# Early loads split by rows, narrower evictions in the first two layers, and a reordered end of a four-layer conditional network

## The reference

```python
# layer 0: a base weight and a low-rank term of all experts, weighted by w = cond_8
out  = einsum('btc,oc->bto', x, W_base) + b_base
h    = einsum('btc,erc->bter', x, As)
x    = x + out + einsum('bter,eor,be->bto', h, Bs, w) * 2.0
# layer 1: a masked weight mixed over the experts
w_bot = einsum('bg,got->bot', cond_8, weight * mask)
x    = x + einsum('bnt,bot->bno', x, w_bot) + bias
# layer 2: gated MLP (128 -> 512 -> 128): one shared, and the top 2 of 8 experts by softmax(cond_8)
x    = x + mlp(x, shared) + sum_k w_k * mlp(x, expert_k)
mlp  = (gelu(x @ gate) * (x @ up)) @ down
# layer 3: gated MLP (128 -> 256 -> 128) of the expert argmax(cond_8)
x    = x + (silu(x @ Wu.T + bu) * (x @ Wg.T + bg)) @ Wd.T + bd
```

## Time and profile before

| what | value |
|---|---|
| three runs, us | 86.94, 88.13, 89.66 (median 88.13) |
| the profiled execution's own time | 87.69 us |
| its span (first to last instruction) | 85.9 us |
| TensorE matmul busy | 82.2 us (96%) |
| TensorE weight load busy | 77.3 us (90%) |
| VectorE, ScalarE, GpSimd busy | 47.3, 30.7, 15.6 us |
| DMA | 18.57 MB, mean 216 GB/s |

### The profile page before, as it was taken

How to read it: one execution, slowest core, us unless ns; L and a number is a source line. 1 busy time by engine, 2 the same in 40 slices (tenths; PEclk the granted TensorE clock), 3 DMA queues, 4 the chain that set the end, 5 groups by cost and what they waited for, 6 DMA issues and landing times.

```text
span 85.9 us, 1918 instructions
## 1 busy us (share of the span) xinstructions
PE 82.2 (96%) x618; PEld 77.3 (90%) x618; DVE 47.3 (55%) x109; ACT 30.7 (36%) x55; POOL 15.6 (18%) x20
## 2 busy tenths in 40 slices
PE   6899999999999999999999999999999999999980
PEld 6788977888888999999999999999999999999970
DVE  0278769743534998329328438446365564563270
ACT  4332692877556420221221221222302402407320
POOL 3020396097666900000000000000000000000000
PEclk9999999999999999999999999999999999999999
DMA  2996006889960000686889889989998979726102
GB/s 12 349 418 256 0 0 183 303 296 402 404 241 10 0 0 4 197 268 272 229 301 342 255 265 346 275 291 331 265 313 309 306 262 323 273 72 154 60 0 61
DMA packets 5479, 18.57 MB, mean 216 GB/s; under 512 B 608, under 2 KB 1888, under 8 KB 5472
## 3 DMA queue, kind: packets, MB, share of 16 engines
q1 hardware_dynamic: 5040, 17.49, 59.9%
q10 hardware_dynamic: 432, 0.98, 2.9%
HBM read 17.95 MB, written 0.52 MB: 215 GB/s over the span
## 4 chain that ended last, share of the span: by engine, by line
PE 87%; DMA 4%; POOL 3%; DVE 2%; issue 1%; DVEq 0%
PE bank L661 33%; PE bank L671 17%; PE bank L684 9%; PE bank L698 4%; PE bank L632 4%; PE bank L641 4%; PE bank L633 4%; DMA first_sb<-in_first 4%; PE bank L581 3%; POOL shared_l L245 3%; PE bank L570 2%; PE bank L649 2%; PE bank L648 2%; PE bank L651 2%; DVE p L377 1%
## 5 line engine op out<-in xcount | busy, mean ns | idle before, releaser
L661 PE MATMUL bank<-x_t,pair_w 128*128 128x128 f32 (+1 forms) x256 | 31.3, 275 | 0.0
L661 PEld LDWEIGHTS bank<-x_t,pair_w 128*128 128x128 f32 x256 | 30.0, 192 | 0.3
L296 ACT ACTIVATE gelu<-bank 128x512 f32<-128x512 f32 x24 | 14.2, 596 | 32.8 <-PE bank L661 28.0
L463 DVE SCALAR_TENSOR_TENSOR hid<-gelu,wsel,bank 128x512 f32<-128x512 f32 x16 | 12.0, 748 | 18.7 <-PE bank L661 18.6
L671 PE MATMUL bank<-hid,pair_w 128*128 128x128 f32 x128 | 16.9, 275 | 0.0
L671 PEld LDWEIGHTS bank<-hid,pair_w 128*128 128x128 f32 x128 | 15.6, 192 | 0.1
L259 POOL TENSOR_TENSOR hid_l<-hid,hid_h 128x512 fp32r<-128x512 f32 x8 | 10.2, 1291 | 4.9 <-ACT hid_h L319 4.9
L461 DVE TENSOR_TENSOR hid<-gelu,bank 128x512 f32<-128x512 f32 x8 | 5.5, 688 | 6.7 <-ACT gelu L296 4.3
L684 PE MATMUL bank<-x_t,w 128*128 128x128 f32 x64 | 8.7, 276 | 0.0
L684 PEld LDWEIGHTS bank<-x_t,w 128*128 128x128 f32 x64 | 7.9, 192 | 0.2 <-issue 0.2
L632 PE MATMUL bank<-x_h,shared_h 128*128 128x512 f32 x16 | 6.4, 401 | 0.1
(11 more groups left out here) (68 smaller groups left out, 74.7 us busy)
## 6 DMA issues: line engine op xcount, KB each, us to landing
pair_w<-in_skill SPq DMA_DIRECT2D x16, 768.0 KB, 5.5
w<-in_layer SPq DMA_DIRECT2D x8, 384.0 KB, 5.2
rest_sb<-in_rest SPq DMA_DIRECT2D x1, 533.0 KB, 4.0
x_t<-in_x SPq DMA_DIRECT2D x1, 512.0 KB, 4.8
shared_sb<-in_shared ACTq DMA_DIRECT2D x1, 512.0 KB, 4.0
out_x<-out_sb SPq DMA_DIRECT2D x8, 64.0 KB, 4.2
shared_sb<-in_shared ACTq DMA_DIRECT2D x1, 256.0 KB, 4.3
first_sb<-in_first ACTq DMA_DIRECT2D x1, 192.0 KB, 3.2
```

Of the source, the lines that this page charges most:

```text
L296: act.activation(gelu[:, n, :], ps[:, :], ACT.Gelu_apprx_tanh).then_inc(gelu_ready, 1)
L463: dve.scalar_tensor_tensor(hid[:, n, :], gelu[:, n, :], wsel[:, bass.DynSlice(weight, 1)], u_ps[n][:, :], ALU.mult, ALU.mult).then_inc(hid ...
L661: mm = pe.matmul(ps[:, S * t:S * (t + 1)], pair_w[:, slot, n, 128 * t:128 * (t + 1)], x2_t[:, columns(b)], start=True, stop=True)
```

## The change

- `first_sb` and `head_sb` are each loaded in two halves of 64 rows, one issued by SP and one by ACT, `first_sb` ahead of `head_sb`; their waits go from 16 to 32.
- Layer 0's result goes to four banks (0, 1, 2, 7), two batches (Q = 256 columns) in each, and ACT evicts it in four quarters; all four stand ahead of the Exp. Layer 1's first half goes to banks 3 and 5 and DVE evicts it in quarters, both of `x2_h` and then both of `x2_t`; its second half stays whole, in bank 4.
- In the shared MLP the products with the low weight are a function of their own, `shared_middle`. For steps 0 and 1 the four high-by-high products stand ahead of the four middle ones; from step 2 on the order stays.
- At the end one chunk of batch 6's up product stands ahead of the last expert's down product and the other behind it; Silu waits for each chunk alone; the bias and the residual of the last two batches are added ahead by ACT (`add_bias3`), so that DVE's last operation has one addition (`result_sum`).

```diff
...
 N = HALF * S
+Q = N // 2
 TOP_K = 2
...
         x3_t = sb("x3_t", [C, 2, S])
+        x3b = sb("x3b", [C, 2, S])
         silu3 = sb("silu3", [128, 2, HC, S])
...
         acc_ps = bank[4]
+        x1_ps = [bank[0], bank[1], bank[2], bank[7]]
+        x2_ps = [bank[3], bank[5]]
         sh_acc = [bank[5], bank[7]]
...
             sem("up3_done"), sem("gate3_done"), sem("half3_ready"), sem("tanh3_ready"), sem("gate3_ready"), sem("hid3_ready"))
-        silu3_ready = sem("silu3_ready")
+        silu3_ready, x3b_ready = sem("silu3_ready"), sem("x3b_ready")
         out_done, out_ready = sem("out_done"), sem("out_ready")
...
         def _(sp):
-            sp.dma_start(head_sb[:, :], head[:, :]).then_inc(head_in, 16)
+            sp.dma_start(first_sb[0:64, :], first[0:64, :]).then_inc(first_in, 16)
+            sp.dma_start(head_sb[0:64, :], head[0:64, :]).then_inc(head_in, 16)
             sp.dma_start(rest_sb[:, :], rest_in[:, :]).then_inc(rest_landed, 16)
...
         def _(act):
-            act.dma_start(first_sb[:, :], first[:, :]).then_inc(first_in, 16)
+            act.dma_start(first_sb[64:128, :], first[64:128, :]).then_inc(first_in, 16)
+            act.dma_start(head_sb[64:128, :], head[64:128, :]).then_inc(head_in, 16)
             act.preload_act_table(ACT.Exp)
-            act.wait_ge(head_in, 16)
+            act.wait_ge(head_in, 32)
             for b in range(HALF, B):
...
-            def stream1(h):
-                act.wait_ge(x1_done, h + 1)
-                act.activation(x1_t[:, N * h:N * (h + 1)], bank[h][:, :], ACT.Identity, bias=b0col).then_inc(x1_ready, 1)
+            def stream1(n):
+                act.wait_ge(x1_done, n + 1)
+                act.activation(x1_t[:, Q * n:Q * (n + 1)], x1_ps[n][:, 0:Q], ACT.Identity, bias=b0col).then_inc(x1_ready, 1)
...
             act.wait_ge(rest_landed, 16)
-            stream1(0)
+            for n in range(4):
+                stream1(n)
             act.wait_ge(shifted_ready, 2)
             act.activation(expo_all[:, :], shifted_all[:, :], ACT.Exp).then_inc(expo_ready, 1)
-            stream1(1)
             round_shared(1)
...
                 for c in range(HC):
-                    act.wait_ge(up3_done, HC * b + (c + 1 if is_last(b) else HC))
+                    act.wait_ge(up3_done, HC * b + c + 1)
                     act.activation(silu3[:, q, c, :], up3_ps(b, c)[:, S * c:S * (c + 1)], ACT.Silu,
                                    bias=bsel[:, c, b:b + 1]).then_inc(silu3_ready, 1)
+            def add_bias3(b, q):
+                act.wait_ge(x3_ready, b + 1)
+                act.activation(x3b[:, q, :], x3_t[:, q, :], ACT.Identity, bias=bsel[:, 2 * HC, b:b + 1]).then_inc(x3b_ready, 1)
...
             silu_step(B - 1, 1)
+            add_bias3(B - 2, 0)
+            add_bias3(B - 1, 1)
...
-            dve.wait_ge(head_in, 16)
+            dve.wait_ge(head_in, 32)
             for first in range(0, HALF, HALF // 2):
...
-            def stream2(h):
-                dve.wait_ge(x2_done, h + 1)
-                dve.wait_ge(x1_ready, h + 1)
-                for dst, done in ((x2_h, x2_high), (x2_t, x2_ready)):
-                    dve.scalar_tensor_tensor(dst[:, N * h:N * (h + 1)], bank[3 + h][:, :], b1col,
-                                             x1_t[:, N * h:N * (h + 1)], ALU.add, ALU.add).then_inc(done, 1)
+            def stream2(dst, done, first, last, ps):
+                dve.wait_ge(x2_done, last)
+                dve.wait_ge(x1_ready, last)
+                dve.scalar_tensor_tensor(dst[:, Q * first:Q * last], ps, b1col, x1_t[:, Q * first:Q * last],
+                                         ALU.add, ALU.add).then_inc(done, last - first)
...
             def stream2_rest(h):
-                dve.wait_ge(x2_ready, h + 1)
+                dve.wait_ge(x2_ready, 2 * (h + 1))
                 dve.tensor_tensor(x2_l[:, N * h:N * (h + 1)], x2_t[:, N * h:N * (h + 1)],
...
-            stream2(0)
+            for dst, done in ((x2_h, x2_high), (x2_t, x2_ready)):
+                for n in range(2):
+                    stream2(dst, done, n, n + 1, x2_ps[n][:, 0:Q])
             stream2_rest(0)
-            stream2(1)
+            for dst, done in ((x2_h, x2_high), (x2_t, x2_ready)):
+                stream2(dst, done, 2, 4, bank[4][:, :])
...
                                          x3_t[:, q, :], ALU.add, ALU.add).then_inc(out_ready, 1)
+            def result_sum(b, q):
+                dve.wait_ge(x3b_ready, b - (B - 2) + 1)
+                dve.wait_ge(stored[q], 16 * (fills(b, q) - 1))
+                dve.wait_ge(out_done, b + 1)
+                dve.tensor_tensor(out_sb[:, q, :], out_bank(b)[:, 0:S], x3b[:, q, :], ALU.add).then_inc(out_ready, 1)
...
             gated_silu3(B - 1, 1)
-            result(B - 2, 0)
-            result(B - 1, 1)
+            result_sum(B - 2, 0)
+            result_sum(B - 1, 1)
...
                     b = HALF * h + n
-                    mm = pe.matmul(bank[h][:, S * n:S * (n + 1)], p0[:, b, :], x_t[:, columns(b)], start=True, stop=True)
-                mm.then_inc(x1_done, 1)
+                    mm = pe.matmul(x1_ps[b // 2][:, S * (b % 2):S * (b % 2 + 1)], p0[:, b, :], x_t[:, columns(b)],
+                                   start=True, stop=True)
+                    if b % 2 == 1:
+                        mm.then_inc(x1_done, 1)
...
                 pe.wait_ge(p1_ready, 2)
-                pe.wait_ge(x1_ready, h + 1)
                 for n in range(HALF):
                     b = HALF * h + n
-                    mm = pe.matmul(bank[3 + h][:, S * n:S * (n + 1)], p1[:, b, :], x1_t[:, columns(b)],
-                                   start=True, stop=True)
-                mm.then_inc(x2_done, 1)
-            pe.wait_ge(first_in, 16)
+                    if n % 2 == 0:
+                        pe.wait_ge(x1_ready, b // 2 + 1)
+                    ps = x2_ps[n // 2][:, S * (n % 2):S * (n % 2 + 1)] if h == 0 else bank[4][:, S * n:S * (n + 1)]
+                    mm = pe.matmul(ps, p1[:, b, :], x1_t[:, columns(b)], start=True, stop=True)
+                    if n % 2 == 1:
+                        mm.then_inc(x2_done, 1)
+            pe.wait_ge(first_in, 32)
             mix1_part(0, EARLY)
-            pe.wait_ge(head_in, 16)
+            pe.wait_ge(head_in, 32)
             mix0(0, HALF // 2, b_mixed, 1)
...
                 if k in (1, 5):
-                    pe.wait_ge(x2_ready, 1 if k == 1 else 2)
+                    pe.wait_ge(x2_ready, 1 if k == 1 else 4)
                 if t == 0:
-                    pe.wait_ge(x2_high, h + 1)
+                    pe.wait_ge(x2_high, 2 * (h + 1))
                 if k == 0:
                     pe.wait_ge(sh_high, m + 1)
+                pe.matmul(ps[:, :], shared_h[:, m, 128 * t:128 * (t + 1)], x2_h[:, N * h:N * (h + 1)], start=True, stop=False)
+            def shared_middle(k, m):
+                h, t = k // T, k % T
+                ps, _ = shared_ps(k, m)
+                if k == 0:
                     pe.wait_ge(sh_low, m + 1)
-                high = x2_h[:, N * h:N * (h + 1)]
-                pe.matmul(ps[:, :], shared_h[:, m, 128 * t:128 * (t + 1)], high, start=True, stop=False)
-                pe.matmul(ps[:, :], shared_l[:, m, 128 * t:128 * (t + 1)], high, start=False, stop=False)
+                pe.matmul(ps[:, :], shared_l[:, m, 128 * t:128 * (t + 1)], x2_h[:, N * h:N * (h + 1)], start=False, stop=False)
...
             shared_high(1, 1)
+            shared_middle(0, 0)
+            shared_middle(0, 1)
+            shared_middle(1, 0)
+            shared_middle(1, 1)
             shared_low(0, 0)
...
             for k in range(2, NSH):
-                for part in (shared_high, shared_low):
-                    for m in range(2):
-                        part(k, m)
+                for m in range(2):
+                    shared_high(k, m)
+                    shared_middle(k, m)
+                for m in range(2):
+                    shared_low(k, m)
                 if k >= 3:
...
             down(B - 1, 0, 1)
-            both_chunks3(B - 2, 0, 0)
+            product3(B - 2, 0, 0, 0)
             down(B - 1, 1, 1)
+            pe.wait_ge(silu3_ready, 1)
+            product3(B - 2, 0, 0, 1)
             both_chunks3(B - 2, 0, 1)
...
```

## The result

The changed kernel takes 88.34 us (median of 22 runs, 87.61 to 90.04) against 87.62 us for the kernel before (22 runs); the ratio is 1.0074, 95% interval 1.0048 to 1.0100. It is slower by about 0.65 us, where 1.1 us faster was forecast. The profiled execution took 88.61 us, its span 86.5 us against 85.9.

A forecast was written before the change was run, and what follows sets the result against it. TensorE, without gaps in the experts' stretch, was taken as the bound, leaving gains only in the first 15 and last 5 us. Transfers 0.23, quarters and order 0.70, end 0.17 sum to 1.10: 87.9 to 86.8 us, range 85.7 to 88.1.

The forecast's parts named there:

- the early transfers: Loads at the start: first_sb lands at 3.46 instead of 3.92, TensorE starts 0.47 us earlier; gain 0.23 us, bounds 0 and 0.47.
- it is the bytes that take time, not the issues: Early loads: the DMA moves a mean of 415 GB/s, so landing times were computed from bytes ahead in the queues.
- `rest_sb` and `x_t` are issued 0.43 later but stand behind the same bytes, and there is slack: Loads behind the halves: later issue costs nothing; TensorE reads rest_sb at 6.9 us against a landing at 5.2.
- `first_sb` at 3.5: Start of TensorE's stream: first product on first_sb at about 3.5 us, its halves having landed at 3.46 instead of 3.92.
- The shared weights are issued after `head_sb` and shift with it, by 0.05: Load of the shared MLP's weights: only 0.05 us later, as head_sb lands at about 3.86 instead of 3.83.
- The quarters and the order: Layers 0 and 1 evicted in quarters, high products first in the shared MLP: gain 0.70 us before the first low product.
- POOL's second low part is late next: Shared MLP: the second middle product waits for POOL, starting at 12.87, 0.14 us behind that part; first low product at 13.63.
- The end: Last products: earlier down product 0.11 us, DVE's last operation with one addition 0.06; sum 0.17 us, bounds 0 and 0.3.
- Rival 4: Early loads: 64-row halves move slower, head_sb lands near 4.75, broken stream may hold 1.2 GHz longer; 88.7 us, chance 0.10.
- its sign of 4.2: Early loads: a head_sb after 4.2 us was named as showing the forecast wrong.
- half a us per us: TensorE's clock at the start: each us longer at 1.2 GHz instead of 2.4 costs 0.5 us.
- the point is fixed in time: TensorE's clock rises from 1.2 to 2.4 GHz between 5.0 and 5.4 us regardless of the stream's start; 0.47 gained becomes 0.23.

The follow-up runs named there:

- with columns: Changed kernel with both early transfers halved by columns, each half with all 128 rows, instead of by rows; ratio 1.0081 to the kernel before.
- the version of the last experiments: Changed kernel with first_sb and head_sb loaded whole and the gate weight's middle products ahead of the up weight's; ratios 0.9925, 0.9999, 0.9872 to the kernel before.

## Why the prediction was wrong

- **The step that failed** stands in the part on the early transfers: "it is the bytes that take time, not the issues", and with it "`rest_sb` and `x_t` are issued 0.43 later but stand behind the same bytes, and there is slack". I took the queue as a pipe that is always full. `rest_sb` was issued 1.07 us later, and the DMA ran at 161 to 256 GB/s from 2.8 to 4.2 us instead of over 380; its busy share there was 0.61 to 1.05, so its engines worked, but on fewer bytes. Up to 3.6 these are largely the 64-row halves of `head_sb`, which the prediction had at no loss beside each other; behind them it is `rest_sb`, whole. `shared_sb` came 2.6 us late. That lateness of `rest_sb` is enough for such a loss is shown by the kernel with `rest_sb` held back; by what path inside the DMA it reaches `shared_sb` stays open, and in the second profile of the changed kernel it was `head_sb` that came late instead. The term was +0.23 us; it measured -1.0 us alone (the halves alone) and about 1.3 us as the difference of the changed kernel and the one with whole loads (1.0074 and 0.9922).
- Inside it, the prices of the issues were wrong: I carried over 0.43 us from whole transfers; halves of 64 rows took 0.57 to 0.88, and `rest_sb`, whole, behind them 0.58 to 0.60.
- The slack of `rest_sb` was counted to TensorE's use of it at 6.9 alone. POOL's `base_i`, which `weights0` needs, used it at 5.34; in the changed kernel `p0` came 0.88 us later, the last 0.55 of its wait for `base_i`, and `product0` 0.14 later.
- `first_sb` at 3.5: it was 3.60, and 3.49 with columns. Right, and worth nothing, since its product waits for `head_sb`'s next.
- "The shared weights are issued after `head_sb` and shift with it, by 0.05": wrong by most of the loss. The row of ACT shows the rounding at 7.82 with the eviction at 9.42 behind it. That was 1.0 us of slack after the rounding, and the prediction asked nothing about the landing of a transfer that is issued into a disturbed queue.
- The quarters and the order: 0.70 forecast, 0.74 measured; ACT's quarter 0.49 forecast, 0.47 measured; DVE's 0.48, and 0.48 measured. "POOL's second low part is late next" came true in the four traces with the changed kernel's order and rounding, with 0.30 to 0.49 us of wait where 0.1 was forecast.
- The end: 0.17 forecast, 0.12 in the trace; of the 0.11 that the reordered products should bring, 0.06 arrived.
- Rival 4 had the mechanism nearest to the truth, a late `head_sb` (4.38 and 5.83 in the two profiles, over its sign of 4.2), and its reason, a slower rate of 64 rows, is seen while `head_sb` moves (199 and 203 against 323 GB/s); the loss by columns comes without it. That its 88.7 lies near the 88.34 measured is luck: most of it was clock that the changed kernel's profiles don't lose, and without that it had a gain of 0.3. Its chance of 0.10 was too small, and that a transfer further back could carry the loss was no rival at all.

## What to carry to other kernels

Before a load is split, look at what is issued behind it on the same queue and who stands behind those landings in another engine's queue; price the issue of the split transfer, and a change of a landing two transfers further on, not only the bytes. Where an engine's queue holds a wait for a load ahead of work that has nothing to do with it, the load's landing is on the path whether the profile of before shows it or not: its slack is the number to read. And two edits that bring nothing alone may bring their whole gain together, so a part that measured zero by itself is not yet a part to drop.

## What the runs showed of the hardware that was not expected

- **Small transfers at the start disturb large ones.** One more transfer of 4 KB on SP's queue took `rest_sb` (533 KB) from 4.0 to 5.4 us; on ACT's queue, 4.2. Of the ten profiles with five or more transfers issued by 3 us, nine have one that took 1.4 to 2.2 us longer than its like, not the same in each (with the tiny one on ACT it was the tiny one itself), and the halves alone one of 1.0. It needs no added transfer: with `rest_sb` only held back, by 0.41 and 1.24 us, `shared_sb` took 5.3 and 5.8 us instead of 4.0. In the changed kernel the last 2 us of the disturbed phase moved 20 to 143 GB/s at a busy share of 0.36 down to 0.05. The cause inside the DMA is not settled by these runs.
- **An issue of half the rows took longer**, 0.57 to 0.88 us against 0.39 to 0.47 for 128 rows among the first transfers, and so did the whole transfer issued right behind such a half (`rest_sb` 0.57 to 0.60, `head_sb` 0.68); the next, `x_t`, took 0.42 to 0.51.
- **TensorE's clock rises at different times from one execution to the next**, and the granted clock doesn't show the rise: it reads 1.00 ahead of it too. The weight loads go from 335 to 192 ns between 5.0 and 5.4 us in the profile of before and between 5.1 and 5.8 in the changed kernel's, but at 4.4 in that of the end alone, by 3.9 with one tiny transfer on SP, and in the profile of the quarters alone more than half of the twelve loads behind `mix0` were still at 333 ns (the columns: shortest, median and longest of them in ns, first and last start in us):

```profile
L599 PEld LDWEIGHTS bank<-first_sb,rest_sb x12: 192/333/337, 7.8 to 10.5; 128*128 128x128 f32 x12
```

There they reach 192 only after 9.9 us, and that execution took 90.25 us, where the seven that the ratio counts took 87.37 to 88.10. The cleanest pair is the version of the last experiments: its first profile has the rise by 5.5 us and `product0` at 8.26 (above), its second has the rise after 9.5 and `product0` at 10.45,

```profile
10.45 1.87 PEld L610 LDWEIGHTS bank<-x_t,p 128*128 128x128 f32 x16
```

with the same transfers issued, and the spans are 84.9 and 87.2 us. So the 1.2 GHz level lasts some 4 us longer in some executions, which costs 2.2 to 2.3 us, more than the whole effect under study. The prediction's half a us per us is borne out; that the point is fixed in time is not: between the profiled executions it lay anywhere from 3.9 to 10 us. It is one reason why single runs of this kernel spread by 3 us; the clock that falls again after TensorE has stood without work, above, is another. How many of the runs without a profile are long for either reason is not shown.
